# AdaLN-conditioned feed-forward block on one core: the two 64-row products at the end of the down projection share the array's two row halves

## The chip, the cores and the metric

The kernel runs on one core of a Trainium2 chip, as one program. The metric is the device time of one execution in microseconds (us); lower is better. Five engines matter. PE (TensorE) multiplies; each matmul needs a weight load (PEld) first. DVE (VectorE), ACT (ScalarE) and POOL (GpSimd) work on rows of up to 128 partitions, and SP issues the transfers. They run side by side and meet at semaphores.

## The reference, cut to what matters

```
# x: (64, 64, 1024) f32; HIDDEN 1024, INTER F = 2752
def fake_quant(t, axis):
    s = max(max(abs(t), axis) / 127, 1e-8)
    return clip(round(t / s), -128, 127) * s

def qlinear(x, w):
    return einsum('bsh,oh->bso', fake_quant(x, -1), fake_quant(w, 1))

y = long_convolution(x) + x * D, masked by length   # filters K from log_dt, C, log_A_real, A_imag
h = silu(qlinear(y, w_gate)) * qlinear(y, w_up)     # (64, 64, 2752)
out = x + qlinear(h, w_down)                        # (64, 64, 1024)
```

## The kernel before

The 4096 rows of x are cut into 32 tiles (`TILES`) of 128 rows. The program has three stages. `long_filters` makes the convolution filters and stores them in DRAM. `convolve_and_pack` convolves one tile per iteration, quantises it and stores it as integers in bf16. In the same iterations it loads the weights, scales and rounds them (ACT L661, L667; POOL L630), transposes them on PE (L868) and lets ACT place them (L675, L680, L683) in `wgu` and `wd`. `feed_forward` then runs over the 32 tiles with all weights in SBUF.

The inner size 2752 is 21 blocks of 128 rows and one of 64, so `FC` is 22 and the last block fills only partitions 0 to 63. The iterations 23 to 30 of `convolve_and_pack` are its down stage, in which `w_down` is prepared, one set of 128 columns of `wd` in each: POOL rounds three pieces (1024, 1024 and 704 columns), PE transposes 8, 8 and 6 blocks (the last one 64 columns wide), and ACT places 8, 8, 5 blocks and then the half one.

In `feed_forward` PE runs for tile t: `gate_up(t, j)` for six pieces j of 512 columns (the last has 192), each as 8 matmuls into `ps_g` and 8 into `ps_u` (L1062), then `down(t - 1)` (L1075). `down` forms two halves o of 512 output columns, one after the other: for each, 22 matmuls of 128x512 accumulate in the bank `ps_o[o]`, the first 21 with 128 rows and the last with 64, which reads partitions 0 to 63 of `h_t` and `wd` (L1086 to L1088). The last matmul of each half increments `down_done`. The order on PE is written out by hand.

DVE scales the two products of piece j (L1113), ACT applies silu (L1175), DVE multiplies them to `h` (L1123) and takes maxima (L1125). After the last piece it forms the scale of the tile (L1130 to L1134). ACT rounds `h` of the tile before during the next tile (L1181), POOL takes off the rounding constant and writes integers to `h_int` (L1216), and SP transposes `h_int` into `h_t` by DMA in six pieces (L1025), which wait for `down_done` of the tile before. DVE's `finish` (L1142, L1145) scales the down product of tile t - 2 after piece 1 of tile t, adds the residual `res`, and SP stores it. POOL clears the last 64 columns of `h_int` once (L1219), and SP waits for that at L1029. The last tile, 31, has no DMA transposes: PE transposes it (L1072), ACT places it (L1190, L1192), and `down(31)` follows.

Of the kernel before, what the change touches and what calls it, by code (L numbers as in the profile page):

```python
# [400 lines left out]
def convolve_and_pack(nc, d, x, w_gate, w_up, w_down, k_rev, xq_dram, s_dram, ident, ones, identb, rounder, mask,  # L401
# [11 lines left out]
    with ExitStack() as ctx:  # L413
        def sb(name, shape, dt=F32):
            return ctx.enter_context(nc.sbuf_tensor(name, shape, dt))
# [4 lines left out]
        def sem(name):  # L420
            return ctx.enter_context(nc.semaphore(name))

        w_int = sb("w_int", [P, F], BF16)
        w_inv = sb("w_inv", [P, 2, 2])
        w_max = sb("w_max", [P, 2])
        w_s = sb("w_s", [P, 2])
# [74 lines left out]
        def down_cols(k):  # L501

            return slice(k * L, min(F, (k + 1) * L))

        def pieces(i, k):

# [109 lines left out]
        @block.gpsimd  # L616
        def _(pool):
            def unround(i, par, k, turned):


                if gate_stage(i):
                    pool.wait_ge(w_rounded, 2 * i + k + 1)
                    src, out = w_f32[:, slot(par, k)][:, ::-1], w_int[:, k * L:(k + 1) * L]
                else:
                    pool.wait_ge(w_rounded, i + GU_UNITS - DOWN_FIRST + 1)
                    cols = down_cols(k)
                    src, out = w_f32[:, down_half(par)][:, cols], w_int[:, cols]
                if turned is not None:
                    pool.wait_ge(w_turned, turned)
                pool.tensor_tensor(out, src, rounder[:].to_broadcast([P, out.shape[1]]),  # L630
                                   ALU.subtract).then_inc(w_int_ready, 1)

            unround(0, 0, 0, None)

            def body(i, par):
                if gate_stage(i):
                    unround(i, par, 1, pieces(i, 1) - 1 if not isinstance(i, int) or i >= 1 else None)
                elif down_stage(i):
                    unround(i, par, 2, pieces(i, 0))
                if not gate_stage(i) and has(i, WEIGHT_ITERS - 1):  # L640
                    unround(i + 1, 1 - par, 0, pieces(i, 0) + 1 if down_stage(i) else GU_UNITS)
                if gate_stage(i) and has(i, GU_ITERS - 1):
                    unround(i + 1, 1 - par, 0, pieces(i, 0) + 1)
                if not gate_stage(i) and has(i, WEIGHT_ITERS - 1):
                    unround(i + 1, 1 - par, 1, pieces(i, 1) + 1 if down_stage(i) else GU_UNITS)

            run(pool, body)

        @block.scalar
        def _(act):  # L650
            def take_u(i, hh):
                act.wait_ge(x_turned, 2 * i + hh + 1)
                if not isinstance(i, int) or i >= 1:
                    act.wait_ge(conv_done, 2 * i + hh - 1)
                act.activation(u[:, hh, :], ps_x[hh][:], ACT.Copy).then_inc(u_done, 1)  # L655

            def round_gu(i, par, u):

                act.wait_ge(w_inv_ready, i + 1)
                cols = slot(par, u)  # L660
                act.activation(w_f32[:, cols], w_f32[:, cols], ACT.Copy, scale=w_inv[:, par, u:u + 1],  # L661
                               bias=ROUND).then_inc(w_rounded, 1)

            def round_down(i, par):
                act.wait_ge(w_inv_ready, weight_turn(i) + 1)
                cols = down_half(par)
                act.activation(w_f32[:, cols], w_f32[:, cols], ACT.Copy, scale=w_inv[:, par, 0:1],  # L667
                               bias=ROUND).then_inc(w_rounded, 1)

            def place_w(i, par, k):  # L670

                act.wait_ge(w_turned, pieces(i, k) + 1)
                if gate_stage(i):
                    dst = wgu[:, :, bass.ds(row_of(i) + k * F, P)]
                    act.activation(dst, ps_w[k][:], ACT.Copy).then_inc(w_placed, 1)  # L675
                    return
                bank = ps_w[(BATCHES * down_slot(par) + k) % 2]
                cols = bass.ds((i - DOWN_FIRST) * P, P)
                whole = min(NC, F // P - NC * k)
                last = act.activation(wd[:, NC * k:NC * k + whole, cols], bank[:, 0:whole, :], ACT.Copy)  # L680
                if k == BATCHES - 1:
                    half = F % P
                    last = act.activation(wd[0:half, FC - 1, cols], bank[0:half, whole, :], ACT.Copy)  # L683
                last.then_inc(w_placed, 1)

            for hh in range(2):
                take_u(0, hh)
            round_gu(0, 0, 0)
            round_gu(0, 0, 1)

            def body(i, par):
                if gate_stage(i):

                    if not isinstance(i, int) or i >= 1:
                        place_w(i - 1, 1 - par, 1)
                elif isinstance(i, int) and i == GU_ITERS:
                    place_w(i - 1, 1 - par, 1)
                if has(i, TILES - 1):
                    take_u(i + 1, 0)
                if not gate_stage(i) and has(i, WEIGHT_ITERS - 1):  # L700
                    round_down(i + 1, 1 - par)
                if gate_stage(i):
                    if has(i, GU_ITERS - 1):
                        round_gu(i + 1, 1 - par, 0)
                elif down_stage(i):
                    place_w(i, par, 0)
                    place_w(i, par, 1)
                if gate_stage(i):
                    place_w(i, par, 0)
                if has(i, TILES - 1):  # L710
                    take_u(i + 1, 1)
                if gate_stage(i):
                    if has(i, GU_ITERS - 1):
                        round_gu(i + 1, 1 - par, 1)
                elif down_stage(i):
                    place_w(i, par, 2)
                if isinstance(i, int) and i == GU_ITERS:
                    act.wait_ge(s_turned, 1)
                    act.activation(s_rows[0:GU_UNITS, :], ps_m[0:GU_UNITS, :], ACT.Copy).then_inc(s_copied, 1)  # L719
                if isinstance(i, int) and i == WEIGHT_ITERS - 1:  # L720
                    act.wait_ge(s_stored, 64)
                    act.wait_ge(s_turned, 2)
                    act.activation(s_rows[0:DOWN_TILES, :], ps_m[0:DOWN_TILES, :], ACT.Copy).then_inc(s_copied, 1)

            run(act, body)
# [103 lines left out]
        def _(pe):  # L829
# [24 lines left out]
            def turn_w(i, par, k):  # L854

                m = pieces(i, k)
                pe.wait_ge(w_int_ready, m + 1)
                if not isinstance(i, int) or m >= 2:

                    pe.wait_ge(w_placed, m - 1)  # L860
                if gate_stage(i):
                    bank, start, stop = ps_w[k], k * L, (k + 1) * L
                else:
                    cols = down_cols(k)
                    bank, start, stop = ps_w[(BATCHES * down_slot(par) + k) % 2], cols.start, cols.stop
                for c, f in enumerate(range(start, stop, P)):
                    width = min(P, stop - f)
                    last = pe.transpose(bank[0:width, c, :], w_int[:, f:f + width], identb[:])  # L868
                last.then_inc(w_turned, 1)

            def turn_max(i):
# [51 lines left out]
def feed_forward(nc, d, x, out, xq_dram, s_dram, identb, rounder, wgu, wd, sx_all, s_gate_up, rows):  # L923
# [15 lines left out]
    with ExitStack() as ctx:  # L939
# [42 lines left out]
        h_int_ready = sem("h_int_ready")  # L982
        h_turned = sem("h_turned")
        h_moved = sem("h_moved")
        h_edge_ready = sem("h_edge_ready")
        h_placed = sem("h_placed")
        down_done = sem("down_done")
        down_scaled = sem("down_scaled")
# [18 lines left out]
        def _(sp):  # L1007
# [18 lines left out]

            sp.dma_start(s_down[:], s_dram[2:3, 0:L].to_broadcast([P, L])).then_inc(s_down_loaded, 16)
            load_res(0)
            sp.wait_ge(h_edge_ready, 1)  # L1029

            def body(t, par):

# [20 lines left out]
        def _(pe):  # L1053
# [21 lines left out]
            def down(t):  # L1075
                last_one = isinstance(t, int) and t == TILES - 1
                if not last_one:
                    pe.wait_ge(h_moved, 16 * PAIRS * t + 16 * PAIRS)
                for o in range(HALVES):
                    if later(t, 1):  # L1080
                        pe.wait_ge(out_ready, HALVES * t - HALVES + o + 1)
                    for c in range(FC):
                        if last_one and o == 0 and c % (W // P) == 0:

                            pe.wait_ge(h_placed, c // (W // P) + 1)
                        width = min(P, F - c * P)  # L1086
                        last = pe.matmul(ps_o[o][:], h_t[0:width, c, :], wd[0:width, c, o * W:(o + 1) * W],  # L1087
                                         start=(c == 0), stop=(c == FC - 1))  # L1088
                    last.then_inc(down_done, 1)

            def body(t, par):
                if later(t, 2):
# [116 lines left out]
        def _(pool):  # L1209
            def unround(t, par, j):  # L1210
                m = PAIRS * t + j
                pool.wait_ge(h_rounded, m + 1)
                if later(t, 1):
                    pool.wait_ge(h_moved, 16 * PAIRS * t)
                n = piece(j).stop - piece(j).start
                pool.tensor_tensor(h_int[:, piece(j)], h[:, par, piece(j)], rounder[:].to_broadcast([P, n]),  # L1216
                                   ALU.subtract).then_inc(h_int_ready, 1)

            pool.memset(h_int[:, F:FC * P], 0.0).then_inc(h_edge_ready, 1)  # L1219

            def body(t, par):

# [64 lines left out]
```

## Time and profile before

| | us |
|---|---|
| median of 3 runs | 1352.94 |
| lowest, highest | 1351.18, 1354.37 |
| profiled execution, its own time | 1353.31 |
| span of that execution in the trace | 1351.2 |
| PE matmuls busy | 1284.5 (95%), 6932 matmuls |
| DVE, ACT, POOL busy | 918.9 (68%), 409.4 (30%), 335.5 (25%) |
| granted PE clock, mean of the span | 0.992 |

The profiled execution's own time is 2.1 us longer than its span, for what lies around it. Busy times overlap, since the engines run side by side. A PE matmul's duration in a row includes its way through the array, so that of two matmuls in a row the second starts before the first ends: what counts for time is the distance between starts. "PEq" and "issue" mean that nothing in the profile held the engine.

### The profile page before, as it was taken

To read this page: it belongs to the slowest core of one execution; us is meant where nothing else is said; L and a number is where in the kernel's file an instruction comes from. 1 tells how busy PE (TensorE), PEld (TensorE's weight loads), DVE (VectorE), ACT (ScalarE), POOL (GpSimd) and SP (SyncE) were. 2 spreads that over 40 slices of the span, in tenths; PEclk is the share of its full clock that TensorE was granted. 3 is DMA by queue.
4 is the path that set the end of the run, shared out by engine and by line. 5 is a ranking of instruction groups with operands and counts; after the bars stand their busy time and mean duration, and the time that the engine had idled before them with its cause. 6 is when DMAs were issued, how large, how long until landed. Compare 5 with 4: busy or idle time off the path is not lost.

```text
span 1351.2 us, 20322 instructions
## 1 busy us (share of the span) xinstructions
PE 1284.5 (95%) x6932; PEld 687.5 (51%) x6932; DVE 918.9 (68%) x1536; ACT 409.4 (30%) x601; POOL 335.5 (25%) x288
## 2 busy tenths in 40 slices
PE   2499999999996999999999999999999999999998
PEld 0377777776663444444444444444444444444443
DVE  7677777778885756676556676566765566765665
ACT  2244454544541322222222222222222222222322
POOL 3333333324440122211212111222112221121220
PEclk9899999999998999999999999999999999999999
DMA  3279999988964122333222332222332233322323
GB/s 97 77 237 269 273 258 269 280 287 239 273 190 154 38 62 68 74 76 83 60 68 68 72 86 67 64 68 70 77 82 60 68 72 76 84 61 66 70 59 78
DMA packets 137594, 161.52 MB, mean 120 GB/s; under 512 B 101644, under 2 KB 101854, under 8 KB 136286
## 3 DMA queue, kind: packets, MB, share of 16 engines
q1 hardware_dynamic: 137566, 161.16, 44.3%
q8 instruction: 16, 0.26, 0.1%
q14 instruction: 12, 0.10, 0.0%
HBM read 113.28 MB, written 25.49 MB: 103 GB/s over the span
## 4 chain that ended last, share of the span: by engine, by line
PE 68%; DVE 0%; ACT 0%; issue 0%
PE ps_o L1087 23%; PE ps_g L1062 22%; PE ps_u L1062 22%; PE ps_t L1072 0%; ACT h_t L1190 0%; DVE ps_o L1142 0%; DVE res L1145 0%
## 5 line engine op out<-in xcount | busy, mean ns | idle before, releaser
L1216 POOL TENSOR_TENSOR h_int<-h,rounder 128x512 bf16<-128x512 f32 x186 | 186.7, 1025 | 698.5 <-ACT h L1181 695.8
L1062 PE MATMUL ps_g<-wgu,rows 128*128 128x512 bf16 (+1 forms) x1536 | 330.8, 359 | 4.5 <-PEq L413 4.5
L1062 PE MATMUL ps_u<-wgu,rows 128*128 128x512 bf16 (+1 forms) x1536 | 329.3, 358 | 0.0
L1087 PE MATMUL ps_o<-wd,h_t 128*128 128x512 bf16 (+1 forms) x1408 | 319.1, 380 | 0.0
L1113 DVE SCALAR_TENSOR_TENSOR g_buf<-ps_g,sx_all,wide 128x512 f32<-128x512 f32 x192 | 132.3, 689 | 242.4 <-PE ps_g L1062 242.4
L1175 ACT ACTIVATE g_buf<-g_buf 128x512 f32<-128x512 f32 x192 | 112.3, 585 | 596.6 <-DVE g_buf L1113 596.6
L850 PE MATMUL ps_y<-u,toep 128*128 128x512 f32 (+7 forms) x1024 | 269.4, 417 | 2.3 <-ACT s_rows L719 1.0
L1062 PEld LDWEIGHTS ps_g<-wgu,rows 128*128 128x128 bf16 x1536 | 145.0, 98 | 163.6 <-issue 13.2
L1087 PEld LDWEIGHTS ps_o<-wd,h_t 128*128 128x128 bf16 (+1 forms) x1408 | 134.2, 98 | 178.0 <-issue 34.4
L1062 PEld LDWEIGHTS ps_u<-wgu,rows 128*128 128x128 bf16 x1536 | 147.0, 98 | 151.8 <-issue 1.3
L850 PEld LDWEIGHTS ps_y<-u,toep 128*128 128x128 f32 x1024 | 177.5, 192 | 89.5 <-issue 58.1
L630 POOL TENSOR_TENSOR w_int<-wide,rounder 128x1024 bf16<-128x1024 f32 (+1 forms) x68 | 127.4, 1884 | 222.2 <-ACT wide L661 160.2
L1113 DVE SCALAR_TENSOR_TENSOR u_buf<-ps_u,sx_all,wide 128x512 f32<-128x512 f32 x192 | 132.4, 690 | 63.5 <-PE ps_u L1062 63.5
L1181 ACT ACTIVATE h<-h,h_inv 128x512 f32<-128x512 f32 x192 | 118.4, 664 | 80.5 <-DVE h_inv L1134 80.5
L1123 DVE TENSOR_TENSOR h<-g_buf,u_buf 128x512 f32<-128x512 f32 x192 | 138.8, 723 | 0.0
L1125 DVE TENSOR_REDUCE h_max<-h 128x1 f32<-128x512 f32 x192 | 121.1, 631 | 6.6
L772 DVE TENSOR_TENSOR y<-ps_y,mask 128x512 f32<-128x512 f32 x64 | 44.1, 689 | 70.8 <-PE ps_y L850 68.4
L655 ACT ACTIVATE u<-ps_x 128x512 f32<-128x512 f32 x64 | 38.1, 597 | 136.3 <-PE ps_x L837 136.3
L661 ACT ACTIVATE wide<-wide,w_inv 128x1024 f32<-128x1024 f32 x44 | 50.2, 1144 | 39.9 <-DVE w_inv L758 39.9
L788 DVE TENSOR_REDUCE y_max<-y 128x128 f32<-128x1024 f32 x32 | 61.6, 1926 | 0.1
L1142 DVE SCALAR_TENSOR_TENSOR ps_o<-ps_o,h_s,s_down 128x512 f32<-128x512 f32 x64 | 48.0, 750 | 9.9 <-DMA res<-in_x 8.3
L1145 DVE TENSOR_TENSOR res<-ps_o,res 128x512 f32<-128x512 f32 x64 | 44.2, 691 | 2.2
(139 smaller groups left out, 618.0 us busy)
## 6 DMA issues: line engine op xcount, KB each, us to landing
toep<-k_rev SPq DMA_DIRECT2D x64, 512.0 KB, 5.7
res<-in_x SPq DMA_DIRECT2D x64, 256.0 KB, 3.8
out_x<-res SPq DMA_DIRECT2D x64, 256.0 KB, 3.2
wide<-in_L_ffn_w_gate SPq DMA_DIRECT2D x22, 512.0 KB, 6.5
wide<-in_L_ffn_w_up SPq DMA_DIRECT2D x22, 512.0 KB, 8.5
wide<-in_L_ffn_w_down SPq DMA_DIRECT2D x8, 1376.0 KB, 8.8
rows<-in_x SPq DMA_DIRECT2D x32, 256.0 KB, 6.5
x_more<-in_x SPq DMA_DIRECT2D x32, 256.0 KB, 7.0
```

The costliest lines, as they stand in the source:

```text
L630: pool.tensor_tensor(out, src, rounder[:].to_broadcast([P, out.shape[1]]), ALU.subtract).then_inc(w_int_ready, 1)
L661: act.activation(w_f32[:, cols], w_f32[:, cols], ACT.Copy, scale=w_inv[:, par, u:u + 1], bias=ROUND).then_inc(w_rounded, 1)
L788: dve.tensor_reduce(y_max[:], y[:, par].rearrange("p c h b -> p (h b) c"), X, ALU.max, apply_absolute_value=True).then_inc(y_max_done, 1)
L850: last = pe.matmul(out[:, dist * B:NC * B], toep[:, slot, block_cols], u[:, hh, 0:n], start=(dist == 0), stop=(dist == NC - 1), skip_group ...
L1062: last = pe.matmul(bank[:, 0:n], xq[:, par, c, :], wgu[:, NC - 1 - c, first + cols.start:first + cols.stop], start=(c == 0), stop=(c == NC ...
L1087: last = pe.matmul(ps_o[o][:], h_t[0:width, c, :], wd[0:width, c, o * W:(o + 1) * W], start=(c == 0), stop=(c == FC - 1))
L1113: dve.scalar_tensor_tensor(out=buf[:, j % 2, 0:n], in0=bank[:, 0:n], scalar=sx, in1=s[:, cols], op0=ALU.mult, op1=ALU.mult).then_inc(gu_sc ...
L1123: dve.tensor_tensor(h[:, par, cols], g_buf[:, j % 2, 0:n], u_buf[:, j % 2, 0:n], ALU.mult).then_inc(h_ready, 1)
L1125: dve.tensor_reduce(h_max[:, par, j:j + 1], h[:, par, cols], X, ALU.max, apply_absolute_value=True).then_inc(h_maxed, 1)
L1175: act.activation(g_buf[:, j % 2, 0:n], g_buf[:, j % 2, 0:n], ACT.Silu).then_inc(silu_done, 1)
L1181: act.activation(h[:, par, cols], h[:, par, cols], ACT.Copy, scale=h_inv[:, par:par + 1], bias=ROUND).then_inc(h_rounded, 1)
L1216: pool.tensor_tensor(h_int[:, piece(j)], h[:, par, piece(j)], rounder[:].to_broadcast([P, n]), ALU.subtract).then_inc(h_int_ready, 1)
```

## The change

The last block is stored twice. POOL writes the last 64 columns of each row once more behind column 2752, into `w_int` (which grows from 2752 to 2816 columns) and into `h_int` (in place of the zeros). The transposes then give partitions 64 to 127 of block 21 the same 64 rows as partitions 0 to 63, in `wd` as in `h_t`. For this the last weight transpose of a set is 128 wide, and ACT places 6 blocks in one instruction where it placed 5 and a half one in two.

`down(t)` for t up to 30 then runs 21 whole blocks for half 0, 21 for half 1, and after them the two 64-row matmuls: half 0's on partitions 0 to 63, half 1's on 64 to 127. Each increments `down_done`. `down(31)` keeps its old form. The clearing of `h_int` and SP's wait for it go.

```
-        w_int = sb("w_int", [P, F], BF16)
+        w_int = sb("w_int", [P, FC * P], BF16)
...
+                if not gate_stage(i) and k == BATCHES - 1:
+                    pool.tensor_tensor(w_int[:, F:FC * P], w_f32[:, down_half(par)][:, F - (FC * P - F):F],
+                                       rounder[:].to_broadcast([P, FC * P - F]), ALU.subtract)
                 pool.tensor_tensor(out, src, rounder[:].to_broadcast([P, out.shape[1]]),
                                    ALU.subtract).then_inc(w_int_ready, 1)
...
-                whole = min(NC, F // P - NC * k)
-                last = act.activation(wd[:, NC * k:NC * k + whole, cols], bank[:, 0:whole, :], ACT.Copy)
-                if k == BATCHES - 1:
-                    half = F % P
-                    last = act.activation(wd[0:half, FC - 1, cols], bank[0:half, whole, :], ACT.Copy)
-                last.then_inc(w_placed, 1)
+                whole = min(NC, FC - NC * k)
+                act.activation(wd[:, NC * k:NC * k + whole, cols], bank[:, 0:whole, :], ACT.Copy).then_inc(w_placed, 1)
...
-                    width = min(P, stop - f)
-                    last = pe.transpose(bank[0:width, c, :], w_int[:, f:f + width], identb[:])
+                    last = pe.transpose(bank[:, c, :], w_int[:, f:f + P], identb[:])
...
+                edge = F - (FC - 1) * P
                 for o in range(HALVES):
                     if later(t, 1):
                         pe.wait_ge(out_ready, HALVES * t - HALVES + o + 1)
-                    for c in range(FC):
+                    for c in range(FC if last_one else FC - 1):
...
-                    last.then_inc(down_done, 1)
+                    if last_one:
+                        last.then_inc(down_done, 1)
+                if not last_one:
+                    for o in range(HALVES):
+                        rows = slice(o * edge, (o + 1) * edge)
+                        pe.matmul(ps_o[o][:], h_t[rows, FC - 1, :], wd[rows, FC - 1, o * W:(o + 1) * W],
+                                  start=False, stop=True).then_inc(down_done, 1)
...
+                if j == PAIRS - 1:
+                    pool.tensor_tensor(h_int[:, F:FC * P], h[:, par, F - (FC * P - F):F],
+                                       rounder[:].to_broadcast([P, FC * P - F]), ALU.subtract)
```

On PE, at the end of a tile in the loop of `feed_forward`, there stands before the change (`ps_u` and `ps_g` are the gate and up products of a tile, `ps_o` the down product; ISA rows are waits):

```order
L1062 MATMUL ps_u<-wgu,rows 128x192 x8
L1078 ISA
L1081 ISA
L1087 MATMUL ps_o<-wd,h_t 128x512 x44
L1093 ISA
L1060 ISA
L1062 MATMUL ps_g<-wgu,rows 128x512 x8
```

and in the changed kernel, at the same place:

```order
L1062 MATMUL ps_u<-wgu,rows 128x192 x8
L1078 ISA
L1082 ISA
L1088 MATMUL ps_o<-wd,h_t 128x512 x42
L1095 MATMUL ps_o<-wd,h_t 128x512 x2
L1100 ISA
L1060 ISA
L1062 MATMUL ps_g<-wgu,rows 128x512 x8
```

Half 0's 64-row matmul has moved from place 22 of the 44 to place 43, next to that of half 1; both stand ahead of the next tile's gate products.

On POOL, in the same loop, the last pieces of a tile read before the change:

```order
L1216 TENSOR_TENSOR h_int<-h,rounder 128x512
L1212 REGISTER_ALU
L1216 TENSOR_TENSOR h_int<-h,rounder 128x192
L1212 ISA
L1214 REGISTER_ALU
```

and in the changed kernel:

```order
L1226 TENSOR_TENSOR h_int<-h,rounder 128x512
L1219 REGISTER_ALU
L1224 TENSOR_TENSOR h_int<-h,rounder 128x64
L1226 TENSOR_TENSOR h_int<-h,rounder 128x192
L1219 ISA
L1221 REGISTER_ALU
```

A 64-column instruction has come between the fifth piece and the last one, behind the wait for the last piece's rounding.

## Rows read from the trace of the kernel before

**Rows 1.** The page: busy us, share of the span and instructions of each engine.
```profile
PE 1284.5 (95%) x6932; PEld 687.5 (51%) x6932; DVE 918.9 (68%) x1536; ACT 409.4 (30%) x601; POOL 335.5 (25%) x288
```

**Rows 2.** Windows (us): busy (count) by engine, granted clock, DMA share, GB/s.
```profile
496.03:1322.59 826.56, 826.56 (x4061) 384.89 (x4060) 535.12 (x900) 203.87 (x349) 174.73 (x174) 1.00 0.30 71
```

**Rows 3.** Timeline, PE of tile 27: start, us, engine, line, operation, count.
```profile
1179.92 9.97 PE L1087 MATMUL ps_o<-wd,h_t 128*128 128x512 bf16 x44
...
1193.29 1.89 PE L1062 MATMUL ps_g<-wgu,rows 128*128 128x512 bf16 x8
...
1207.10 0.82 PE L1062 MATMUL ps_g<-wgu,rows 128*128 128x192 bf16 x8
...
1208.42 0.38 PE L1087 MATMUL ps_o<-wd,h_t 128*128 128x512 bf16 x1
```

**Rows 4.** Timeline in narrow windows, PE, around half 0's 64-row matmul.
```profile
1184.02 0.59 PE L1087 MATMUL ps_o<-wd,h_t 128*128 128x512 bf16 x2
...
1184.55 0.39 PE L1087 MATMUL ps_o<-wd,h_t 64*128 64x512 bf16 x1
...
1184.86 0.39 PE L1087 MATMUL ps_o<-wd,h_t 128*128 128x512 bf16 x1
...
1185.09 0.38 PE L1087 MATMUL ps_o<-wd,h_t 128*128 128x512 bf16 x1
```

**Rows 5.** Groups by form, L1087's 64-row weight load: busy, mean ns, idle before.
```profile
L1087 PEld LDWEIGHTS ps_o<-wd,h_t 64*128 64x128 bf16 x64 | 5.9, 93 | 27.1 <-issue 27.1
```

**Rows 6.** Timeline, filter stage, windows of 5 and 15 ns: matmuls on the two row halves.
```profile
42.10 0.26 PE L391 MATMUL ps_k<-wgu 64*32 64x32 f32 x1 [12.20 <-DVE wgu L301]
...
42.10 0.26 PE L391 MATMUL ps_k<-wgu 64*32 64x32 f32 x2 [12.20 <-DVE wgu L301]
```

**Rows 7.** Timeline, PE, down stage: 6 transposes, then 16, and what follows each.
```profile
346.08 0.61 PE L868 MATMUL ps_w<-identb,w_int 128*128 128x128 bf16 x6
346.62 4.21 PE L850 MATMUL ps_y<-u,toep 128*128 128x512 f32 x16
...
352.33 1.07 PE L868 MATMUL ps_w<-identb,w_int 128*128 128x128 bf16 x16
353.23 1.08 PE L850 MATMUL ps_y<-u,toep 128*128 128x512 f32 x2
```

**Rows 8.** Waits of PE in the down stage, 312 to 408 us: total, times, longest.
```profile
PE ps_m L873 <- DVE y_max L788: 2.9, 5, 0.6
```

**Rows 9.** Groups by form, POOL.
```profile
L1216 POOL TENSOR_TENSOR h_int<-h,rounder 128x512 bf16<-128x512 f32 x155 | 158.9, 1042 | 698.5 <-ACT h L1181 695.8 <-DMA h_t<-h_int 2.7
...
L630 POOL TENSOR_TENSOR w_int<-wide,rounder 128x1024 bf16<-128x1024 f32 x60 | 113.7, 1902 | 222.2 <-ACT wide L661 160.2 <-ACT wide L667 61.9
...
L1216 POOL TENSOR_TENSOR h_int<-h,rounder 128x192 bf16<-128x192 f32 x31 | 29.1, 939 | 0.0
```

**Rows 10.** Timeline, tile 28: DVE and POOL at piece 0, then bank ps_g0's reuse.
```profile
1197.32 1.95 POOL L1216 TENSOR_TENSOR h_int<-h,rounder 128x512 bf16<-128x512 f32 x2 [1.32 <-ACT h L1181]
1197.61 1.29 DVE L1123 TENSOR_TENSOR h<-g_buf,u_buf 128x512 f32<-128x512 f32 x1
...
1202.32 0.74 DVE L1113 SCALAR_TENSOR_TENSOR g_buf<-ps_g,sx_all,wide 128x512 f32<-128x512 f32 x1
...
1203.43 0.53 PEld L1062 LDWEIGHTS ps_g<-wgu,rows 128*128 128x128 bf16 x3
```

**Rows 11.** Timeline, SP of tile 28: the six DMA transposes.
```profile
1189.97 10.89 SPq L1025 DMA_TRANSPOSE h_t<-h_int  x6
```

**Rows 12.** Timeline, the tail: DVE's finish of tiles 30 and 31.
```profile
1331.28 0.75 DVE L1142 SCALAR_TENSOR_TENSOR ps_o<-ps_o,h_s,s_down 128x512 f32<-128x512 f32 x1
...
1332.33 0.62 PE L1072 MATMUL ps_t<-identb,h_int 128*128 128x128 bf16 x8
...
1342.49 0.76 DVE L1142 SCALAR_TENSOR_TENSOR ps_o<-ps_o,h_s,s_down 128x512 f32<-128x512 f32 x1 [8.34 <-DMA res<-in_x]
1345.50 0.76 DVE L1142 SCALAR_TENSOR_TENSOR ps_o<-ps_o,h_s,s_down 128x512 f32<-128x512 f32 x1 [1.52 <-PE ps_o L1087]
```

More of the change, by code:

```diff
@@ L503, in down_cols, with turn_cols @@
             return slice(k * L, min(F, (k + 1) * L))
+        def turn_cols(k):
+            return slice(k * L, min(FC * P, (k + 1) * L))
         def pieces(i, k):
@@ L863, in turn_w @@
                 else:
-                    cols = down_cols(k)
+                    cols = turn_cols(k)
                     bank, start, stop = ps_w[(BATCHES * down_slot(par) + k) % 2], cols.start, cols.stop
                 for c, f in enumerate(range(start, stop, P)):
-                    width = min(P, stop - f)
-                    last = pe.transpose(bank[0:width, c, :], w_int[:, f:f + width], identb[:])
+                    last = pe.transpose(bank[:, c, :], w_int[:, f:f + P], identb[:])
                 last.then_inc(w_turned, 1)
@@ L984, in feed_forward @@
         h_moved = sem("h_moved")
-        h_edge_ready = sem("h_edge_ready")
         h_placed = sem("h_placed")
@@ L1028, in _ @@
             load_res(0)
-            sp.wait_ge(h_edge_ready, 1)
             def body(t, par):
@@ L1215, in unround @@
                 n = piece(j).stop - piece(j).start
+                if j == PAIRS - 1:
+                    pool.tensor_tensor(h_int[:, F:FC * P], h[:, par, F - (FC * P - F):F],
+                                       rounder[:].to_broadcast([P, FC * P - F]), ALU.subtract)
                 pool.tensor_tensor(h_int[:, piece(j)], h[:, par, piece(j)], rounder[:].to_broadcast([P, n]),
                                    ALU.subtract).then_inc(h_int_ready, 1)
-            pool.memset(h_int[:, F:FC * P], 0.0).then_inc(h_edge_ready, 1)
             def body(t, par):
```

## The prediction

> **What bounds the kernel now.** Start with the busy times [rows 1]: PE 95%, DVE 68%, the rest under a third. That is an average over stages, so the windows come next [rows 2]: from 496 to 1323 us, which is `feed_forward` from its second down product to its last ones, PE is busy for every one of 826.56 us, at a clock of 1.00. No wait of PE is left in there. What a piece of work costs on PE in this stage is therefore read from the distance between starts, and a saving on PE counts in full as long as the engine that is next stays ahead of it.
>
> **The base rate.** In the tile that follows this down product, there are from the gate matmuls of piece 1 to those of piece 5 64 matmuls of 128x512, in 1207.10 - 1193.29 = 13.81 us, so 0.2158 us from start to start [rows 3]. One tile takes 1208.42 - 1179.92 = 28.50 us [rows 3].
>
> **What a 64-row matmul costs.** From the start of the down product to piece 1 there are 44 + 16 = 60 matmuls in 1193.29 - 1179.92 = 13.37 us [rows 3]. At the base rate they would take 12.95. The two 64-row matmuls thus cost 0.42 us more than their slots, 0.21 each. The narrow windows show where [rows 4]: the two whole matmuls before start at 1184.02 and 1184.23 (0.59 long together, 0.38 each), the 64-row one at 1184.55, the next whole ones at 1184.86 and 1185.09. The distances are 0.32, 0.31 and 0.23 where 0.216 is normal: about 0.10 on entering the 64-row form, 0.10 on leaving it and 0.01 after it. In both places the weights are not loaded ahead; the 64-row load has 27.1 us of idle time before it in 64 cases [rows 5].
>
> **The change in `feed_forward`.** It touches tiles 0 to 30, 31 times.
> - Removed: one entry and exit, 0.21 us, since the two 64-row matmuls now stand side by side and only one pair of switches is left.
> - Removed if they run at once: one slot, 0.216 us.
> - Left: the delay of the second behind the first. The nearest rows are in this kernel's filter stage, where matmuls alternate between partitions 0 to 63 and 64 to 127 with different output banks, as here. One takes 0.26 us, and the first two together, seen within 15 ns, take 0.26 as well [rows 6]. Two whole-array ones of 0.38 take 0.59 [rows 4]. So the second starts within about 0.01 us. It is the first pair after an idle time, with its own weight loads, so loads don't hold it back either. Bounds: 0 below, one slot (0.216) above if they don't run at once. I take 0.01, by the row. What keeps me from certainty: those are 64x32 f32 matmuls, far shorter than a 64x512 one.
>
> The tile then saves 0.21 + 0.216 - 0.01 = 0.416 us, and 31 tiles 12.9 us. Between the bounds it is 0.21 to 0.426 us, or 6.5 to 13.2 us.
>
> The Trainium skill (TensorE: Matmul & The Clock Gate, "Part 3: Packing small matmuls") says that increments of a semaphore by every tile of a packed group are made one after the other, 26.3 ns each. The pair has two. As an estimate from that page, if PE had to sit this out, 31 x 0.026 = 0.8 us would go from the gain and 12.1 would be left. No row here shows PE waiting for an increment, so the sum leaves it out.
>
> **Is the next engine ahead?** Three places could hold PE once it is 0.42 us faster per tile.
> - The transposes of `h_t`. They begin at `down_done`, which comes at the end of the down product both before and after, at 1189.97, and their issues end 10.89 us later [rows 11]. PE needs them at 1208.42 [rows 3], 7.6 us later; most of what lies between is gate work, which doesn't shrink. Cost nothing.
> - The extra POOL instruction, one per tile. From 512 to 1024 columns POOL's time rises from 1.042 to 1.902 us, 1.68 ns a column [rows 9], so 64 columns cost 1.042 - 448 x 0.00168 = 0.29 us. Bounds: 0.13 (an eighth of 1.04) and 0.94, what the 192-column one shows with its waits [rows 9]. POOL is busy a quarter of the time, and only the sixth transpose waits for it, with the slack just named. Cost nothing on POOL itself. What it can do to DVE is a rival, below.
> - `finish` of tile t - 2 runs after piece 1 of tile t. That it gets half 0 later doesn't matter there, since both halves were done before the gate work of tile t began.
>
> **The tail.** Here half 0's later end does matter. Tile 30's `finish` starts at 1331.28, 1.05 us before PE's transposes start at 1332.33 [rows 12]. With both halves ready only at the end of `down(30)` it starts about 1.15 us later against PE, and so do its store, the load of the new residual and tile 31's half 0, which waits for that load (8.34 us) until 1342.49 [rows 12]. Half 0 then takes 0.76 + 0.69 + about 0.05 and would end near 1345.15 on the same scale; half 1 has to wait for PE until 1345.50 anyway [rows 12]. Slack 0.35 us: cost nothing, and if the cover is gone, 0.3 us or so.
>
> **The weight stage.** In the 8 iterations of the down stage the last transpose is now 128 wide. 6 transposes take 346.62 - 346.08 = 0.54 us to the next convolution, 16 all-wide ones 353.23 - 352.33 = 0.90, 0.056 each, so 6 would take 0.34 [rows 7]. PE gains 0.20 us per iteration, 1.6 in all. But PE then waits for DVE's `y_max` in five or six of the 8 iterations, up to 0.6 us long [rows 8], and a PE that comes earlier waits longer. I count two iterations, 0.4 us. ACT gives up one of two instructions and isn't late there. The extra POOL instruction stands between two others that DVE competes with; if DVE lost 0.29 us to it in six iterations, 1.7 us would be lost. Bounds: -1.7 to +1.6.
>
> **Sum.** 12.9 + 0.4 = 13.3 us. The profiled execution goes from 1353.31 to 1340.0. The median before is 0.37 us lower, 1352.94, which gives 1339.6.
>
> **The rivals.**
> 1. The second half's weights are loaded only when the first matmul has begun. A 64-row load takes 93 ns [rows 5]. The second matmul then starts 0.09 to 0.10 us late: 31 x 0.09 = 2.8 us less gain, 1342.4. For it: on entering the form, loads aren't made ahead [rows 4]. Against it: the filter stage's first pair.
> 2. The matmuls don't overlap, because they are long and both stream 512 columns. Then only a switch pair is saved, 0.21 x 31 + 0.4 = 6.9 us: 1346.0. For it: in the filter stage short matmuls could look concurrent by their starts alone.
> 3. The change doesn't do what it says: the two follow each other, and going from the lower to the upper half costs a switch of 0.10 us as well. Then one switch of four is saved, 0.11 x 31 + 0.4 = 3.8 us: 1349.1.
> 4. Slower, by DVE. At piece 0 DVE's product, which reads two tiles, and POOL stood in each other's way: it took 1.29 us from 1197.61, and POOL's fifth piece, begun at 1197.32 and 1.04 long, ended at 1198.36, so 0.75 us were blocked and 0.54 worked [rows 9, 10]. It got in between the fifth and sixth piece. Were it to lose that place and wait for the 64- and the 192-column instruction too, it would lose 0.29 + about 0.50 us, at the bounds 0.94 + 0.50 = 1.44. The delay goes on through `finish` to the scaling of piece 2, which ends at 1202.32 + 0.74 = 1203.06 and frees the bank for the load at 1203.43 [rows 10]. That load is made one slot ahead of its matmul and takes 0.10, so PE loses from 1203.55 on: slack 0.49 us. With 0.79 PE would lose 0.30 per tile, less than it gains. The case decides the sign from a delay of 0.49 + 0.43 = 0.92 us; at 1.44 PE loses 0.95 per tile, 29.5 us, and the kernel takes 1369. Against it: DVE already won the place between two POOL pieces, and the order of requests is unchanged.
>
> The Trainium skill (SBUF — State Buffer, "Who interferes with whom") calls the shared port pair an exclusive lock and says that DVE with two SBUF inputs and a POOL instruction that reads SBUF block each other fully. The 1.29 us agree [rows 10]. By that rule every added POOL read is a place at which DVE can be late; it doesn't say who comes first when both wait.
>
> **How the numbers follow.** Forecast 0.80; rival 1 0.08; rival 2 0.06; rival 3 0.02; rival 4 0.04. The predicted time is the forecast's. Its own bounds are the weight stage's (-2.1, +1.2 against the 0.4 taken) and half of the spread of runs before (1351.18 to 1354.37), about 1.5: 1337 to 1342.5. Rival 1 belongs in the range with the same uncertainty, up to 1344. Faster or slower by 0.2% (2.7 us) is about what a measurement of this kernel can tell from no change; forecast and rivals 1 and 2 are all faster by more, and half of rival 3: 0.95. Its other half and a little of rival 4 are the same: 0.02. The rest of rival 4: 0.03.
>
> **What would show it.** Right: the pair's two rows start within about 0.01 us in the changed trace, once per tile, and the next whole matmul starts 0.31 after them; the down product to piece 1 takes 12.95 us instead of 13.37; a tile takes 28.08 us; PE stays at 100% from the second down product on. Rival 1 shows 0.1 between the pair, rival 2 0.22, rival 3 0.31. Rival 4 shows waits of PE's gate loads on DVE's scaling at piece 4, and longer products in DVE's piece 0. In the weight stage the convolution follows the transposes after 0.34 us and PE waits longer for `y_max`. In the tail, a half 1 of tile 31 that waits for DVE and not for PE would cost a few tenths.

## The result, and the profile after

The changed kernel takes 1339.14 us (median of 5 runs, 1338.46 to 1340.08), against 1352.94 before: a ratio of 0.9902, 95% interval 0.989 to 0.9914. That is 13.8 us less, where 13.3 were forecast. The forecast of 1339.6 us is 0.5 us off. The profiled execution has a span of 1336.9 us.

The page shows almost the same shares as [rows 1]; PE's count is lower than that of its weight loads because some matmul records are missing from this trace.

```profile
PE 1263.6 (95%) x6837; PEld 686.5 (51%) x6932; DVE 918.1 (69%) x1536; ACT 409.0 (31%) x593; POOL 345.0 (26%) x326
```

The timeline of PE in tile 27, to be laid beside [rows 3] (start, us, engine, line, operation, count), and then the pair in two narrow windows, the first 6 ns wide:

```profile
1168.16 9.23 PE L1088 MATMUL ps_o<-wd,h_t 128*128 128x512 bf16 x41
1177.32 0.39 PE L1095 MATMUL ps_o<-wd,h_t 64*128 64x512 bf16 x2
1177.65 1.90 PE L1062 MATMUL ps_g<-wgu,rows 128*128 128x512 bf16 x8
...
1181.11 1.89 PE L1062 MATMUL ps_g<-wgu,rows 128*128 128x512 bf16 x8
...
1196.24 4.05 PE L1088 MATMUL ps_o<-wd,h_t 128*128 128x512 bf16 x18
```

```profile
1177.32 0.39 PE L1095 MATMUL ps_o<-wd,h_t 64*128 64x512 bf16 x1
...
1177.32 0.39 PE L1095 MATMUL ps_o<-wd,h_t 64*128 64x512 bf16 x2
```

One tile takes 1196.24 - 1168.16 = 28.08 us where it took 28.50. From the down product to piece 1 there are 1181.11 - 1168.16 = 12.95 us, before 13.37. The two 64-row matmuls take 0.39 us together, as long as one: the second starts less than 0.01 us after the first. The next whole matmul starts 0.33 us after the pair's start by these rounded rows, where 0.31 was forecast.

Over the whole stage it adds up. In the second trace of the changed kernel (below), whose records around tile 31 are complete, the first and the last down product start at these times (the first two rows are of the kernel before, the last two of the changed one):

```profile
467.36 9.97 PE L1087 MATMUL ps_o<-wd,h_t 128*128 128x512 bf16 x44
...
1335.48 9.98 PE L1087 MATMUL ps_o<-wd,h_t 128*128 128x512 bf16 x44
```

```profile
466.26 9.23 PE L1088 MATMUL ps_o<-wd,h_t 128*128 128x512 bf16 x42
...
1321.29 9.98 PE L1088 MATMUL ps_o<-wd,h_t 128*128 128x512 bf16 x44
```

1321.29 - 466.26 = 855.03 us against 1335.48 - 467.36 = 868.12, so 13.09 us less in 31 tiles, 0.422 each. PE also stays busy throughout, as in [rows 2]; the window of that trace from the second down product on:

```profile
494.34:1308.50 814.16, 814.16 (x4062) 384.70 (x4060) 534.64 (x900) 203.80 (x348) 182.18 (x203) 1.00 0.30 72
```

The rest of the 13.8 lies ahead of this stage or in the scatter of runs: the kernel `more_switches` below has the front of the kernel before, word for word, and still reached its first down product at 465.23, 2.1 us earlier than the kernel before did. The median of the kernel before was also 1353.30 and 1353.71 us in the two sets of runs beside the experiments.

POOL and DVE in the changed kernel, groups by form (busy, mean ns | idle before), to be laid beside [rows 9]:

```profile
L1226 POOL TENSOR_TENSOR h_int<-h,rounder 128x512 bf16<-128x512 f32 x155 | 158.9, 1042 | 706.2 <-ACT h L1188 703.4 <-DMA h_t<-h_int 2.7
...
L1130 DVE TENSOR_TENSOR h<-g_buf,u_buf 128x512 f32<-128x512 f32 x160 | 127.6, 798 | 0.0
...
L1224 POOL TENSOR_TENSOR h_int<-h,rounder 128x64 bf16<-128x64 f32 x31 | 22.5, 725 | 0.0
L1226 POOL TENSOR_TENSOR h_int<-h,rounder 128x192 bf16<-128x192 f32 x31 | 15.5, 500 | 0.0
```

The 192-column piece fell from 939 to 500 ns. The wait for DVE that it carried has moved to the new 64-column instruction, which now stands ahead of it and shows 725 ns. DVE's product has a mean of 798 ns, and in the trace of before the same group had 127.6 us and 798 ns too.

### The profile page after: what moved, and what is told of

It reads as the page before. It is cut to its first block, busy times and chain, and to the rows that moved or that the text cites. A ratio compares the mean times of both kernels' runs of the same rounds, so it can differ in the third digit from the quotient of the medians.

```text
span 1336.9 us, 20250 instructions
## 1 busy us (share of the span) xinstructions
PE 1263.6 (95%) x6837; PEld 686.5 (51%) x6932; DVE 918.1 (69%) x1536; ACT 409.0 (31%) x593; POOL 345.0 (26%) x326
## 4 chain that ended last, share of the span: by engine, by line
PE 67%; issue 0%; DVE 0%; ACT 0%
PE ps_g L1062 23%; PE ps_u L1062 22%; PE ps_o L1088 22%; PE ps_o L1095 1%; PE ps_t L1072 0%; ACT h_t L1197 0%; DVE ps_o L1149 0%; DVE res L1152 0%
## 5 line engine op out<-in xcount | busy, mean ns | idle before, releaser
L1226 POOL TENSOR_TENSOR h_int<-h,rounder 128x512 bf16<-128x512 f32 x186 | 174.4, 952 | 706.2 <-ACT h L1188 703.4
L1062 PE MATMUL ps_g<-wgu,rows 128*128 128x512 bf16 (+1 forms) x1516 | 327.1, 358 | 5.9 <-PEq L413 4.9
L1062 PE MATMUL ps_u<-wgu,rows 128*128 128x512 bf16 (+1 forms) x1493 | 324.4, 356 | 2.3
L1088 PE MATMUL ps_o<-wd,h_t 128*128 128x512 bf16 x1314 | 294.0, 379 | 1.8 <-issue 0.2
L1088 PEld LDWEIGHTS ps_o<-wd,h_t 128*128 128x128 bf16 x1346 | 131.1, 98 | 151.9 <-issue 1.1
L637 POOL TENSOR_TENSOR w_int<-wide,rounder 128x1024 bf16<-128x1024 f32 (+1 forms) x68 | 124.6, 1838 | 219.6 <-ACT wide L668 159.4
```

The costliest lines, as they stand in the source:

```text
L1062: last = pe.matmul(bank[:, 0:n], xq[:, par, c, :], wgu[:, NC - 1 - c, first + cols.start:first + cols.stop], start=(c == 0), stop=(c == NC ...
```

## Experiments

The theory going in: a 64-row product between whole ones costs its slot of 0.216 us plus 0.21 us for entering and leaving the 64-row form (a switch pair), and the change saves one slot and one switch pair per tile. Each ratio below is against the kernel before as it ran beside that experiment. The rivals: it is adjacency alone, or overlap alone, or something in the wider storage; and on the other side, that POOL and DVE take something back.

### Both products on the lower half: `adjacent`

```
-                        rows = slice(o * edge, (o + 1) * edge)
+                        rows = slice(0, edge)
```

> The changed kernel, but both 64-row products read partitions 0 to 63, one after the other at the end of the down product of tiles 0 to 30 (same values, output unchanged). Theory (a gain of two parts per tile: one pair of switches, 0.21 us, and one slot, 0.216 us): only the switches are saved. The down product to piece 1 takes 13.16 us, the second 64-row matmul starts 0.216 us after the first, the kernel gains 31 x 0.21 = 6.5 us on before (ratio 0.995), half of the change. Rival (adjacency alone makes the gain, overlap is nothing): ratio 0.990, like the changed kernel. Rival (the extra cost belongs to each 64-row matmul, wherever it stands, and the gain is all overlap): ratio 1.000.

1345.39 us, ratio 0.9946 (0.9932 to 0.9959). PE, timeline, two tiles in a row:

```profile
1144.87 9.23 PE L1088 MATMUL ps_o<-wd,h_t 128*128 128x512 bf16 x41
1154.03 0.60 PE L1095 MATMUL ps_o<-wd,h_t 64*128 64x512 bf16 x2
...
1173.16 9.23 PE L1088 MATMUL ps_o<-wd,h_t 128*128 128x512 bf16 x41
1182.33 0.60 PE L1095 MATMUL ps_o<-wd,h_t 64*128 64x512 bf16 x2
1182.86 1.90 PE L1062 MATMUL ps_g<-wgu,rows 128*128 128x512 bf16 x8
```

The pair takes 0.60 us instead of 0.39, and the tile 1173.16 - 1144.87 = 28.29 us. That is 0.21 less than before and 0.21 more than changed: half of the gain is the switches, half the overlap. Both rivals of this run are out.

### The two halves, but not neighbours: `apart`

```
-                    for c in range(FC if last_one else FC - 1):
+                    for c in range(FC):
...
+                        rows = slice(0, min(P, F - c * P))
+                        if not last_one and c == FC - 1:
+                            rows = slice(o * edge, (o + 1) * edge)
...
```

> The changed kernel, but with the 64-row products back in their old places, half 0's on the lower row half at place 22, half 1's on the upper row half at place 44. Theory: nothing of the down product's gain is left, since no two 64-row products are neighbours; the down product to piece 1 takes 13.37 us, the kernel is within 1 us of before (what is left is the weight stage's few tenths), ratio 0.9995. Rival (the upper half or the wider storage by itself brings something): ratio under 0.998.

1351.92 us, ratio 0.9993 (0.9984 to 1.0002), no difference that could be measured.

```profile
1150.98 9.97 PE L1090 MATMUL ps_o<-wd,h_t 128*128 128x512 bf16 x43
1179.48 9.97 PE L1090 MATMUL ps_o<-wd,h_t 128*128 128x512 bf16 x43
```

28.50 us per tile, as before. The upper half and the double storage bring nothing by themselves. All of the down product's gain needs the two to be neighbours. The run also bounds by times alone what the weight stage's edits bring: 0.9 us by the ratio, and by the interval anything from 2.2 us gained to 0.3 lost.

### More 64-row products: `more_switches`

```
-                        width = min(P, F - c * P)
+                        width = min(P, F - c * P) if last_one or c != 10 else F % P
```

> The kernel before, with block 10 of each half of the down product of tiles 0 to 30 cut to its first 64 rows (the other 64 rows of that block are left out), so there are four 64-row products per tile, each between whole ones, and still 44 products. Theory (each isolated 64-row product costs 0.21 us on top of its slot): the tile takes 28.50 + 0.42 = 28.92 us, the kernel 1352.9 + 13.1 = 1366 us, ratio 1.0097. Rival (the cost belongs to the end of an accumulation, to its semaphore increment or to the change of bank, which fall together with the 64-row product in the kernel before): ratio 1.000.

1364.44 us against 1353.71 for the kernel before beside it, ratio 1.0086 (1.0069 to 1.0103).

```profile
1159.31 10.39 PE L1087 MATMUL ps_o<-wd,h_t 128*128 128x512 bf16 x44
1188.23 10.39 PE L1087 MATMUL ps_o<-wd,h_t 128*128 128x512 bf16 x44
```

The same 44 products, two more of them with half the rows, and the tile takes 28.92 us instead of 28.50, the 0.42 that was expected. The cost belongs to the change of form and not to the end of an accumulation, the bank or the semaphore: block 10 has none of these. The total came out 1.6 us under the expected 1366, and the front of this run was 2.1 us early, as said above.

### No 64-row product at all: `padded`

The kernel before with the last block filled up with zeros, in both integer tiles, and every product and transpose over the whole array.

```
-        w_int = sb("w_int", [P, F], BF16)
+        w_int = sb("w_int", [P, FC * P], BF16)
...
+            pool.memset(w_int[:, F:FC * P], 0.0)
...
-                        width = min(P, F - c * P)
-                        last = pe.matmul(ps_o[o][:], h_t[0:width, c, :], wd[0:width, c, o * W:(o + 1) * W],
+                        last = pe.matmul(ps_o[o][:], h_t[:, c, :], wd[:, c, o * W:(o + 1) * W],
```

> No 64-row products at all: the last block is filled up with zeros in w_int and h_int, written once, and all 44 products of every tile, tile 31 too, are whole-array ones; no extra POOL instruction. Theory (a switch pair costs 0.21, a whole product 0.216 us): 44 slots without switches, 9.50 us, against 43 slots, 0.004 and one switch pair, 9.49, so this is as fast as the changed kernel, and 0.42 us better in tile 31: ratio 0.990, down product to piece 1 12.95 us. Rival (overlap is worth more than the row distances say, or whole products on zeros cost more): slower than the changed kernel by over 2 us, ratio 0.992 or more.

1338.54 us, ratio 0.9889 (0.9874 to 0.9904).

```profile
1140.79 9.66 PE L1086 MATMUL ps_o<-wd,h_t 128*128 128x512 bf16 x43
1168.88 9.66 PE L1086 MATMUL ps_o<-wd,h_t 128*128 128x512 bf16 x43
1178.37 1.89 PE L1062 MATMUL ps_g<-wgu,rows 128*128 128x512 bf16 x8
```

28.09 us per tile in these rows, 28.08 in the next tile (1196.96 - 1168.88); one of the 44 records is missing. Multiplying 64 rows of zeros is as fast as the pair. It needs no second copy, no extra POOL instruction and no upper half, and it also helps tile 31. Its interval overlaps that of the changed kernel, so which of the two is faster isn't known; neither beats the other by what could be measured.

### The extra POOL instruction: `no_pool` and `six_pool`

`no_pool` takes it out and zeroes the columns once:

```
-                if j == PAIRS - 1:
-                    pool.tensor_tensor(h_int[:, F:FC * P], h[:, par, F - (FC * P - F):F],
-                                       rounder[:].to_broadcast([P, FC * P - F]), ALU.subtract)
...
+            pool.memset(h_int[:, F:FC * P], 0.0).then_inc(h_edge_ready, 1)
```

> The changed kernel without the extra POOL instruction per tile in the feed-forward stage: the last 64 columns of h_int are zeroed once, so half 1's 64-row product multiplies zeros and the contribution of the last block to output columns 512 to 1023 is left out for tiles 0 to 30. It measures what the instruction costs. Theory: nothing, it hides behind PE; same time as the changed kernel within 1 us. Rival (DVE is held up by it and PE now and then by DVE): 1 to 9 us faster than the changed kernel.

`six_pool` adds five:

```
+        spare = sb("spare", [P, 10, 64], BF16)
...
+                    for k in range(5):
+                        pool.tensor_tensor(spare[:, 5 * par + k], h[:, par, F - (FC * P - F):F],
+                                           rounder[:].to_broadcast([P, FC * P - F]), ALU.subtract)
```

> The changed kernel with six POOL instructions of 64 columns per tile where it has one, the five others into a spare tile (output unchanged). It tests the rival of a slower kernel by DVE. Theory (DVE gets in as soon as the POOL piece that was running ends, and PE is covered): POOL's pieces end some 1.5 us later per tile, DVE's product at piece 0 still takes 1.3 us, and the time is that of the changed kernel within 1 us, 1339. Rival (DVE has to let all POOL pieces pass): DVE's product takes about 2.7 us, PE waits for the bank at piece 4 by about 0.9 us per tile, 1367 us.

1338.88 us without it (ratio 0.9897, 0.9881 to 0.9912) and 1338.26 with six (0.989, 0.9873 to 0.9906): the count of POOL instructions, 0, 1 or 6, makes no difference. `six_pool`, POOL and DVE at piece 0 of a tile:

```profile
1186.25 1.04 POOL L1230 TENSOR_TENSOR h_int<-h,rounder 128x512 bf16<-128x512 f32 x1 [1.32 <-ACT h L1189]
1187.25 0.74 POOL L1225 TENSOR_TENSOR h_int<-h,rounder 128x64 bf16<-128x64 f32 x1
1187.95 1.29 POOL L1228 TENSOR_TENSOR spare<-h,rounder 128x64 bf16<-128x64 f32 x5
1189.21 0.50 POOL L1230 TENSOR_TENSOR h_int<-h,rounder 128x192 bf16<-128x192 f32 x1
...
1186.55 1.29 DVE L1131 TENSOR_TENSOR h<-g_buf,u_buf 128x512 f32<-128x512 f32 x1
```

```profile
L1228 POOL TENSOR_TENSOR spare<-h,rounder 128x64 bf16<-128x64 f32 x155 | 40.4, 291 | 0.0
...
L1131 DVE TENSOR_TENSOR h<-g_buf,u_buf x169: 347/679/1298, 512.6 to 1298.9; 128x512 f32<-128x512 f32 x141, 128x192 f32<-128x192 f32 x28
```

DVE's product began at 1186.55, while POOL's fifth piece ran. It took 1.29 us as in [rows 10], though seven POOL instructions stood behind that piece. DVE went first when the running one ended, and the 64-column instruction that came next carries the wait (0.74 us where the five behind it show 0.29 each). That is one tile; of the 169 products of DVE from 512.6 to 1298.9 us the longest took 1298 ns (shortest, median and longest stand in the last row), so none waited for a second POOL instruction. With a product of the same length as before, DVE was at the bank in time, and the tile still takes 28.08 us (down products at 1141.20 and 1169.28).

### The whole down product in pairs: `all_pairs`

```
+                    for c in range(FC - 1):
+                        for turn in range(2):
+                            for o in range(HALVES):
+                                side = o
+                                rows = slice(side * edge, (side + 1) * edge)
+                                pe.matmul(ps_o[o][:], h_t[rows, c, :], wd[rows, c, o * W:(o + 1) * W],
+                                          start=(c == 0 and turn == 0), stop=False)
```

> The changed kernel, but the whole down product of tiles 0 to 30 runs as pairs on the two row halves: 43 pairs of 64-row products, half 0's always on the lower and half 1's always on the upper half, in the order lower, upper. For the blocks 0 to 20 half 0 multiplies only the lower 64 rows (twice) and half 1 only the upper 64 (twice), so half of each block's contribution is left out and the other counted double; the number of products and their sizes are what a full product in this form would need. Theory (a pair takes one slot, with its weight loads made ahead): 43 slots and one switch pair, the tile takes 28.08 us as in the changed kernel, 1339 us. Rival (the weight loads of a pair can't be made ahead of it, or two streams of 512 columns can't be kept up): at least 0.09 us more per pair, 43 x 0.09 = 3.9 us per tile, 1460 us or more.

1339.74 us (ratio 0.9901, 0.9882 to 0.9921, from two runs).

```profile
702.18 1.90 PE L1062 MATMUL ps_g<-wgu,rows 128*128 128x512 bf16 x8
...
720.88 9.24 PE L1089 MATMUL ps_o<-wd,h_t 64*128 64x512 bf16 x84
729.95 0.38 PE L1106 MATMUL ps_o<-wd,h_t 64*128 64x512 bf16 x2
730.26 1.90 PE L1062 MATMUL ps_g<-wgu,rows 128*128 128x512 bf16 x8
```

86 products of 64 rows in 43 slots: the 42 pairs of the first row and the last pair lie (729.95 - 720.88) / 42 = 0.216 us apart, and the tile takes 730.26 - 702.18 = 28.08 us. Within the 64-row form the weight loads, two per slot of 94 ns each, cost PE no time, and two streams of 512 columns are kept up over all 43 pairs. What costs is only the way in and out.

### Once more, beside these: `changed_again`

> The changed kernel as it is, on the same chip and in the same rounds as the others of this call, for comparison. 1339 us, ratio 0.990.

1338.9 us, ratio 0.9896 (0.988 to 0.9913).

The runs as one table; the tile's time is worked out from starts in the traces:

| kernel | slots per tile | switch pairs | us per tile | median us | ratio |
|---|---|---|---|---|---|
| before | 44 | 2 | 28.50 | 1352.94 | 1 |
| changed | 43 | 1 | 28.08 | 1339.14 | 0.9902 |
| `adjacent` | 44 | 1 | 28.29 | 1345.39 | 0.9946 |
| `apart` | 44 | 2 | 28.50 | 1351.92 | 0.9993 |
| `padded` | 44 | 0 | 28.08 | 1338.54 | 0.9889 |
| `more_switches` | 44 | 4 | 28.92 | 1364.44 | 1.0086 |
| `all_pairs` | 43 | 1 | 28.08 | 1339.74 | 0.9901 |

With 0.216 us for a slot and 0.21 for a switch pair every row of the column "us per tile" comes out within 0.01 us, counted from `padded`.

## Why the prediction was right, point by point

**What bounds the kernel.** PE did, and a saving on it counted in full: 0.422 us per tile on PE are 13.09 us over the stage, and PE is busy for all of 814.16 us from the second down product on.

**The switch pair, 0.21 us.** Right, and shown twice, by taking one away (`adjacent`) and by adding two (`more_switches`).

**The slot and the delay of the second, 0.216 - 0.01.** Right; the delay is below 0.01 us. The doubt that was named, that short f32 products say little on long ones, is settled by the pair's rows and by `all_pairs`. With 0.422 measured against 0.416 forecast, the stage's term was 13.1 and not 12.9. The smaller sum that one could form from the increments of `down_done` (the Trainium skill, TensorE: Matmul & The Clock Gate, "Part 3: Packing small matmuls") was not what happened: the pair ends with two increments, and the tile shows nothing of 0.026 us. Whether the second increment reaches those who wait for it later, no run here was made to show.

**Transposes and POOL at no cost.** Right. The 64-column instruction was priced at 0.29 us from the slope between two sizes, and the 155 of `six_pool` that stand free show 291 ns. No wait of PE stands in the changed trace between 470 and 1300 us.

**The tail.** Right, it cost nothing. In the changed kernel DVE's `finish` of tiles 30 and 31 reads, beside [rows 12]:

```profile
1318.22 0.76 DVE L1149 SCALAR_TENSOR_TENSOR ps_o<-ps_o,h_s,s_down 128x512 f32<-128x512 f32 x1 [0.70 <-PE ps_o L1095]
...
1329.52 0.76 DVE L1149 SCALAR_TENSOR_TENSOR ps_o<-ps_o,h_s,s_down 128x512 f32<-128x512 f32 x1 [8.43 <-DMA res<-in_x]
...
1331.21 0.76 DVE L1149 SCALAR_TENSOR_TENSOR ps_o<-ps_o,h_s,s_down 128x512 f32<-128x512 f32 x1 [0.21 <-PE ps_o L1088]
```

DVE now waits 0.70 us for the pair at tile 30, and at tile 31's half 1 it still waits for PE, for 0.21 us where it was 1.52: that is what was left of the cover, against 0.35 forecast. In the second trace of the changed kernel this wait was 0.33 us, so the forecast lies within what two traces differ by.

**The weight stage, 0.4 us.** Less than half of that, and this is the term that was mis-sized. The wide transpose itself is 0.2 us faster on the way to the next convolution, as priced: PE, timeline of the changed kernel, beside [rows 7].

```profile
345.51 0.51 PE L870 MATMUL ps_w<-identb,w_int 128*128 128x128 bf16 x6
345.85 4.16 PE L853 MATMUL ps_y<-u,toep 128*128 128x512 f32 x16
350.63 0.30 PE L875 MATMUL ps_m<-ident,y_max 128*128 128x128 f32 x1 [0.61 <-DVE y_max L791]
```

From 0.54 to 0.34 us. How much of it arrives is read from one matmul, the one that takes up `y_max` in every iteration. Here it is in the kernel before at the start of the stage, at its first wait for `y_max`, at its last one, and behind the stage:

```profile
316.30 0.28 PE L873 MATMUL ps_m<-ident,y_max 128*128 128x128 f32 x1
...
351.45 0.30 PE L873 MATMUL ps_m<-ident,y_max 128*128 128x128 f32 x1 [0.62 <-DVE y_max L788]
...
400.42 0.30 PE L873 MATMUL ps_m<-ident,y_max 128*128 128x128 f32 x1 [0.54 <-DVE y_max L788]
...
419.88 0.33 PE L873 MATMUL ps_m<-ident,y_max 128*128 128x128 f32 x1 [2.41 <-DVE y_max L788]
```

and in the changed kernel (the second one, at 350.63, stands above):

```profile
315.48 0.28 PE L875 MATMUL ps_m<-ident,y_max 128*128 128x128 f32 x1
...
399.57 0.30 PE L875 MATMUL ps_m<-ident,y_max 128*128 128x128 f32 x1 [0.79 <-DVE y_max L791]
...
418.90 0.33 PE L875 MATMUL ps_m<-ident,y_max 128*128 128x128 f32 x1 [2.41 <-DVE y_max L791]
```

From the first to the second there are 35.15 us before and 35.15 after, from the second to the third 48.97 and 48.94, from the third to the fourth 19.46 and 19.33. The whole is 103.58 and 103.42 us, 0.16 less. This repeats: `more_switches`, which has the old weight stage, takes 103.59, and the kernels with the wide transpose take 103.40 to 103.44. Only `adjacent` takes 103.70, with a wait of 1.28 us for a load of x. So of 1.6 us that PE gained, the end got 0.16.

What failed is the step that let each iteration without a wait pass its gain on to the end (two were counted). PE had no wait in the first iterations, but it came early to the next wait for `y_max` and waited longer there (or, in this trace, 0.66 us for a load of x). Only the last set of transposes, with no such wait close behind it, passed something on, 0.13 us. PE's waits for `y_max` in the window of [rows 8] rose from 2.9 to 3.6 us, and to 4.3 in the second trace. The extra POOL instruction took nothing from DVE in this stage: `padded`, which has none, takes 103.43, and the loss of 1.7 us that stood as a bound didn't come. On the total of 13.3 the error is 0.2 us, far below what a comparison of times can tell.

**The rivals.** The late weight load (0.09 us per pair) and the missing overlap are excluded by the pair's rows, a switch between the halves too. The slower case needed DVE to let all waiting POOL instructions pass; `six_pool` gave it the best conditions, and it didn't occur. The Trainium skill (SBUF — State Buffer, "Who interferes with whom") calls the shared port pair an exclusive lock, and the 1.29 us agree. It names no case in which one engine has more work waiting behind the instruction that holds the lock; here DVE, whose product had begun at 1186.55, went ahead of POOL's next instruction, which began at 1187.25. The median product took 679 ns, so being blocked cost the long one 0.61 us, where the prediction read 0.75; the rival's price doesn't hang on it.

## What to carry to other kernels

Where PE is the bound, count the changes between whole-array products and those with fewer rows, not only the products: at 512 columns one odd product costs nearly as much again, 0.21 us on 0.216. Put the odd ones next to each other, on different row halves and banks if the data can be there; or, if only a few are odd, fill them up with zeros, which here was as fast with less code. By these prices the two ways tie only for a single pair: 0.216 + 0.21 us against two slots, 0.432. As an estimate, each further pair beside the first would cost one slot where filled products cost two; no run here compares the two ways with more odd products. Check for each saving which later step was already waiting: on PE's full stretch all of it arrived, in the stage with waits for DVE a tenth, since the next wait took back what came before it.

## What the runs showed of the hardware

- Products of 64 rows on partitions 0 to 63 and 64 to 127, into different banks, run at the same time, and 43 pairs in a row keep a distance of 0.216 us, the same as whole ones.
- Going in and out costs 0.21 us together at a granted clock of 1.00. At both changes the weight load starts only about when its matmul does (1184.55 and 1184.86 in [rows 4]), where the load at 1184.02 was made a slot ahead of the matmul at 1184.23. Whether the late load is the cause of the 0.21 us or goes along with it, no run here separates. The weight loads of the kernel before, at the same place:

```profile
1184.02 0.10 PEld L1087 LDWEIGHTS ps_o<-wd,h_t 128*128 128x128 bf16 x1
1184.54 0.09 PEld L1087 LDWEIGHTS ps_o<-wd,h_t 64*128 64x128 bf16 x1 [0.42 <-issue]
1184.86 0.55 PEld L1087 LDWEIGHTS ps_o<-wd,h_t 128*128 128x128 bf16 x4 [0.23 <-issue]
```

- Between two products on the same half there is no second switch (`adjacent`: 0.60 us for two, 0.59 for two whole ones [rows 4]).
- When a DVE product of two SBUF inputs waited for a POOL instruction to end, it went ahead of POOL's next one, with seven still to come (`six_pool`: 1.29 us, and at most 1298 ns in 169 products).
- The convolution and weight stages scatter by about 2 us from trace to trace with the same code (first down product at 467.36 in the kernel before and 465.23 in `more_switches`), more than anything the change did there. The scatter isn't in the down stage, which takes 103.58 and 103.59 us in these two.
